# Attention stage: gathered sums copied by ScalarE in two parts, reciprocals on VectorE, multiply on GpSimd

## What is computed

```python
    x = x + _L1_attn_ref(_layernorm(x, axis=-1), L1_attn_w_qkv, L1_attn_w_out, L1_attn_b_out)

    def _L1_attn_ref(x, w_qkv, w_out, b_out):
        ...
        q = q * cos + rotate_half(q) * sin
        k = k * cos + rotate_half(k) * sin
        scale = hd ** (-0.5)
        dots = jnp.einsum('bhid,bhjd->bhij', q, k) * scale
        attn = jax.nn.softmax(dots, axis=-1)
        out = jnp.einsum('bhij,bhjd->bhid', attn, v)
        out = out.transpose(0, 2, 1, 3).reshape(b, n, H * hd)
        return out @ w_out + b_out
```

## Time and profile before

| | |
|---|---|
| median of 3 runs | 2716.94 us |
| lowest and highest | 2711.95 and 2725.21 us |
| profiled execution | 2727.38 us |
| its span | 2725.5 us |
| attention stage, first reduction to last multiply | 979.4 to 1660.0 us |
| busy over the whole span: TensorE, VectorE, ScalarE, GpSimd | 81%, 72%, 52%, 35% |
| largest-value reductions (L2054) | 512, 1.218 us each |
| exponentials (L1918) | 1024, 0.597 us each |

### The profile page before, as it was taken

The page is one execution under the profiler, slowest core; times in us unless marked ns, Lnnn a source line. Parts: engine busy times, 40 slices in busy tenths (PEclk is TensorE's granted clock), DMA queues, the critical chain, the costliest instruction groups (busy, mean ns, idle before and its releaser), DMA issues. The chain is left out here.

```text
span 2725.5 us, 48018 instructions
## 1 busy us (share of the span) xinstructions
PE 2215.1 (81%) x15540; PEld 1397.6 (51%) x15540; DVE 1950.6 (72%) x4482; ACT 1415.7 (52%) x2887; POOL 947.8 (35%) x1183
## 2 busy tenths in 40 slices
PE   3399788876968769999999997959767697698986
PEld 3299577765865312232322323659746686533334
DVE  4466588875656579999999982756567565688893
ACT  2166221214645449989899883336542464533333
POOL 4644335453442321111111100754427444223330
PEclk9999798887989969999999996969978798899998
DMA  5122101001221130000000000112211123100001
GB/s 164 46 58 65 44 18 30 16 22 44 64 82 40 65 128 23 22 20 22 21 21 23 21 3 33 39 51 66 74 44 40 54 63 88 46 0 0 1 0 32
DMA packets 110499, 115.42 MB, mean 42 GB/s; under 512 B 21776, under 2 KB 93552, under 8 KB 109488
## 3 DMA queue, kind: packets, MB, share of 16 engines
q1 hardware_dynamic: 91936, 76.13, 9.8%
q0 software_dynamic: 17280, 35.69, 3.9%
q10 hardware_dynamic: 1040, 0.53, 0.1%
HBM read 67.30 MB, written 44.57 MB: 41 GB/s over the span
## 5 line engine op out<-in xcount | busy, mean ns | idle before, releaser
L2054 DVE TENSOR_REDUCE attn_nm<-bank 128x1 f32<-128x1024 f32 x512 | 592.5, 1218 | 27.2 <-PE bank L1796 24.8
L1918 ACT ACTIVATE attn_pT<-bank 128x512 f32<-128x512 f32 x1024 | 554.3, 597 | 77.3 <-PE bank L1812 70.9
L1831 PE MATMUL bank<-attn_pT,attn_vb 128*32 128x256 f32 x4096 | 334.8, 399 | 10.0 <-issue 10.0
L1796 PE MATMUL bank<-attn_K,attn_Q 48*128 48x512 bf16 x1024 | 317.5, 391 | 23.5 <-PEq L1530 16.7
L1812 PE MATMUL bank<-attn_Q,attn_K 51*128 51x512 bf16 x1024 | 324.5, 390 | 2.0 <-DMA attn_Q<-attn_m_parts 2.0
L1998 POOL CAST attn_m_cols<-attn_nm 128x8 bf16<-128x8 f32 x64 | 12.2, 190 | 483.5 <-DVE attn_nm L2054 455.9
L1831 PEld LDWEIGHTS bank<-attn_pT,attn_vb 128*32 128x32 f32 x4096 | 83.0, 109 | 189.6 <-issue 142.4
L1796 PEld LDWEIGHTS bank<-attn_K,attn_Q 48*128 48x128 bf16 x1024 | 59.4, 94 | 231.1 <-DVE attn_nm L2054 142.8
L2816 POOL TENSOR_TENSOR mix_rS<-mix_rT,mix_S 128x512 f32<-128x512 f32 x64 | 82.7, 1292 | 171.3 <-DVE mix_S L2871 84.4
L1017 PE MATMUL bank<-mix_prod_qk,ident 128*128 128x256 f32 x512 | 124.6, 400 | 0.0
L1017 PEld LDWEIGHTS bank<-mix_prod_qk,ident 128*128 128x128 f32 x512 | 104.4, 204 | 31.8 <-issue 17.7
(11 more groups left out here) (619 smaller groups left out, 5671.2 us busy)
## 6 DMA issues: line engine op xcount, KB each, us to landing
w<-in_L_w SPq DMA_DIRECT2D x4, 2048.0 KB
ffn0a_x_ring<-xs_rows SPq DMA_DIRECT2D x71, 65.0 KB
ffn0b_x_ring<-xs_rows SPq DMA_DIRECT2D x71, 65.0 KB
ffn2a_x_ring<-xs_rows SPq DMA_DIRECT2D x71, 65.0 KB, 1.8
ffn2b_x_ring<-xs_rows SPq DMA_DIRECT2D x71, 65.0 KB, 1.8
mix_in_y_back<-y_rows SPq DMA_DIRECT2D x8, 512.0 KB, 4.0
ffn1a_in_y_back<-y_rows SPq DMA_DIRECT2D x8, 512.0 KB, 4.4
ffn2a_y_back<-y_rows SPq DMA_DIRECT2D x8, 512.0 KB, 3.9
```

Source lines behind the costliest of these rows:

```text
L1796: ins = nc.tensor.matmul(out[:, hf, :], slot(net.Q, h, 0, KROWS)[:, qt * P:(qt + 1) * P], slot(net.K, h, 0, KROWS)[:, hf * CH:(hf + 1) * C ...
L1831: ins = nc.tensor.matmul(pv_bank[at:at + VCOL, cols], vb[:, h, kt, :], q[:, cols], start=(opens(h) and pair == 0 and half == 0), stop=(clo ...
L1918: nc.scalar.activation(pT[:, p_at(b, h, kt), hf * CH:(hf + 1) * CH], s_bank(n), ACT.Exp, scale=HD ** -0.5).then_inc(s_used, 1)
L2054: nc.vector.tensor_reduce(nm[:, v % NMRING, qt:qt + 1], a_bank(n).rearrange("p a t -> p (a t)"), AX.X, ALU.max, negate=True).then_inc(a_us ...
```

## The change

The gather goes in two parts of two tiles each, one at the fifth and one at the sixth tile row, each into a bank of the ring of three (`s_place`) instead of a pair of `big`'s banks. ScalarE copies each part, 128x108, to SBUF (`keep_sums`, into the new tile `gathered`). VectorE takes only the reciprocals, from SBUF, behind the eighth reduction of the head (`invert`, `INVERT_AT` 7). GpSimd multiplies (`over`), behind the split of the maxima and ahead of its other work of that head. `turn_o` waits for GpSimd's multiply. Each step of the sequence's end moves to the next head: 1 and 2, 3 and 4, 4 and 5, 4 and 6, 5 and 7, 6 and 8 where it was 0 and 1, 2 and 3, 3 and 4, 3 and 5, 4 and 6, 5 and 7. The diff, cut to the core; the same shift of heads stands in the programs of TensorE and ScalarE, too:

```diff
--- before.py
+++ after.py
@@ -1646,7 +1646,7 @@
-        TURN_AT, GATHER_AT, END_AT = 4, 4, 6
+        TURN_AT, GATHER_AT, END_AT = 4, (4, 5), 6
@@ -1654,7 +1654,10 @@
-        rd = part.sb("rden", [P, 2, TPB, HEADS_SUMMED])
+        INVERT_AT = GATHER_AT[-1] + 2
+        rd = part.sb("rden", [P, TPB, HEADS_SUMMED])
+        TILES_PART, SUMS_W = TPC // len(GATHER_AT), HPB * SUM_COLS
+        gathered = part.sb("gathered", [P, len(GATHER_AT), TILES_PART * SUMS_W])
@@ -1733,16 +1736,17 @@
-                if kt == GATHER_AT and u > 0 and closes((u - 1) % H):
-                    a_place["sums", *divmod(u - 1, H)] = len(a_place)
+                if kt in GATHER_AT and u > 0 and closes((u - 1) % H):
+                    s_place["sums", *divmod(u - 1, H), GATHER_AT.index(kt)] = len(s_place)
...
-                    if h in (0, 1):
-                        s_place["o", b - 1, h] = len(s_place)
-                    if h in (2, 3):
-                        a_place["y", b - 1, h - 2] = len(a_place)
-                    if h in (5, 7):
-                        s_place["xn", b - 1, h // 7] = len(s_place)
-        a_place["sums", B - 1, H - 1] = len(a_place)
+                    if h in (1, 2):
+                        s_place["o", b - 1, h - 1] = len(s_place)
+                    if h in (3, 4):
+                        a_place["y", b - 1, h - 3] = len(a_place)
+                    if h in (6, 8):
+                        s_place["xn", b - 1, h // 8] = len(s_place)
+        for part_no in range(len(GATHER_AT)):
+            s_place["sums", B - 1, H - 1, part_no] = len(s_place)
@@ -1834,21 +1838,21 @@
-            def gather(b, h):
+            def gather(b, h, part_no):
...
-                if done == 1:
+                if done == 1 and part_no == 0:
...
-                out = take_a(a_place["sums", b, h])
-                W = HPB * SUM_COLS
-                for i in range(TPC):
-                    ins = nc.tensor.matmul(out[:, 0, i * W:(i + 1) * W], sums[:, i * P:(i + 1) * P],
+                out = take_s(s_place["sums", b, h, part_no])
+                for j in range(TILES_PART):
+                    i = part_no * TILES_PART + j
+                    ins = nc.tensor.matmul(out[:, j * SUMS_W:(j + 1) * SUMS_W], sums[:, i * P:(i + 1) * P],
...
-                ins.then_inc(a_ready, 1)
+                ins.then_inc(s_ready, 1)
...
-                pe.wait_ge(a_used, a_place["sums", b, H - 1] + 1)
+                pe.wait_ge(over_step, (b + 1) * len(SPANS))
@@ -1897,14 +1901,15 @@
-                        if kt == GATHER_AT and last and closes(last[1]):
-                            gather(*last)
+                        if kt in GATHER_AT and last and closes(last[1]):
+                            gather(*last, GATHER_AT.index(kt))
...
-            gather(B - 1, H - 1)
+            for part_no in range(len(GATHER_AT)):
+                gather(B - 1, H - 1, part_no)
@@ -1929,8 +1934,15 @@
-                    act.wait_ge(a_ready, a_place["sums", *divmod(u, H)] + 1)
+                    act.wait_ge(s_ready, s_place["sums", *divmod(u, H), len(GATHER_AT) - 1] + 1)
...
+
+            def keep_sums(b, h, part_no):
+                n = s_place["sums", b, h, part_no]
+                need(act, over_step, closed(b * H + h) - 1)
+                act.wait_ge(s_ready, n + 1)
+                nc.scalar.activation(gathered[:, part_no, :], s_bank(n)[:, 0:TILES_PART * SUMS_W],
+                                     ACT.Copy).then_inc(s_used, 1)
@@ -1977,10 +1989,14 @@
+                        if kt in GATHER_AT and last and closes(last[1]):
+                            keep_sums(*last, GATHER_AT.index(kt))
...
+            for part_no in range(len(GATHER_AT)):
+                keep_sums(B - 1, H - 1, part_no)
@@ -2002,16 +2018,27 @@
+            def over(b, h):
+                g, at, size = span(h)
+                pool.wait_ge(inverted, closed(b * H + h))
+                if g == 0 and b > 1:
+                    pool.wait_ge(s_ready, s_place["o", b - 2, HPB - 1] + 1)
+                pv = gathered[:].rearrange("p a (t s e) -> p (a t) s e", s=HEADS_SUMMED, e=V1)[:, :, 0:size]
+                first = first_of[g] * HD
+                nc.gpsimd.tensor_tensor(o[:, b % 2, :, first:first + size * HD].rearrange("p t (s d) -> p t s d", d=HD),
+                                        pv[:, :, :, 0:HD], bcast(rd[:, :, 0:size].rearrange("p t (s a) -> p t s a", a=1),
+                                                                     [P, TPB, size, HD]), ALU.mult).then_inc(over_step, 1)
+
...
-                if h in (2, 3):
-                    add_bias(b, h - 2)
-                if h in (3, 5):
-                    norm.rstd_pow(pool, chunk(b, h // 5))
+                if h in (3, 4):
+                    add_bias(b, h - 3)
+                if h in (4, 6):
+                    norm.rstd_pow(pool, chunk(b, h // 6))
@@ -2054,37 +2084,26 @@
-            def over(b, h):
-                g, at, size = span(h)
-                n = a_place["sums", b, h]
-                chain = Chain(dve, over_step, closed(b * H + h) - 1)
-                dve.wait_ge(a_ready, n + 1)
-                if g == 0 and b > 1:
-                    dve.wait_ge(s_ready, s_place["o", b - 2, HPB - 1] + 1)
-                pv = a_bank(n)[:, 0, 0:TPC * HPB * SUM_COLS].rearrange(
-                    "p (t s e) -> p t s e", s=HEADS_SUMMED, e=V1)[:, :, 0:size]
-                rden = rd[:, g % 2, :, 0:size]
-                chain.then(nc.vector.reciprocal(rden, pv[:, :, :, HD]))
-                chain.wait()
-                first = first_of[g] * HD
-                nc.vector.tensor_tensor(o[:, b % 2, :, first:first + size * HD].rearrange("p t (s d) -> p t s d", d=HD),
-                                        pv[:, :, :, 0:HD],
-                                        bcast(rden.rearrange("p t (s a) -> p t s a", a=1), [P, TPB, size, HD]),
-                                        ALU.mult).then_inc(a_used, 1)
+            def invert(b, h):
+                size, done = span(h)[2], closed(b * H + h)
+                need(dve, over_step, done - 1)
+                dve.wait_ge(s_used, s_place["sums", b, h, len(GATHER_AT) - 1] + 1)
+                pv = gathered[:].rearrange("p a (t s e) -> p (a t) s e", s=HEADS_SUMMED, e=V1)[:, :, 0:size]
+                nc.vector.reciprocal(rd[:, :, 0:size], pv[:, :, :, HD]).then_inc(inverted, 1)
...
-                if qt == END_AT and h in (2, 3):
-                    c, n = chunk(b, h - 2), a_place["y", b, h - 2]
+                if qt == END_AT and h in (3, 4):
+                    c, n = chunk(b, h - 3), a_place["y", b, h - 3]
...
-                if qt == 2 and h in (3, 4):
-                    c = chunk(b, h - 3)
+                if qt == 2 and h in (4, 5):
+                    c = chunk(b, h - 4)
...
-                if qt == 1 and h in (4, 6):
-                    norm.apply(dve, chunk(b, h // 6))
+                if qt == 1 and h in (5, 7):
+                    norm.apply(dve, chunk(b, h // 7))
@@ -2096,12 +2115,12 @@
-                        if qt == GATHER_AT and last and closes(last[1]):
-                            over(*last)
+                        if qt == INVERT_AT and last and closes(last[1]):
+                            invert(*last)
...
-            over(B - 1, H - 1)
+            invert(B - 1, H - 1)
...
```

33 lines of the change are left out of this document (18 added, 15 removed).

## The result

| | before | after |
|---|---|---|
| median of 10 runs each | 2720.77 us | 2734.66 us |
| lowest and highest | 2711.95 and 2727.32 us | 2724.36 and 2737.88 us |
| ratio after to before | | 1.0037, interval 1.0022 to 1.0052 |
| profiled execution, its span | 2727.38, 2725.5 us | 2736.86, 2735.0 us |

The changed kernel is slower by 0.37%, between 0.22% and 0.52%. That is less than the 0.5% within which I had called it the same, but it is not zero: 10 us by this ratio, with 6 to 14 us as its interval. I had worked out 6.7 us.

The account below looks back on a forecast made before the run. The prediction took TensorE's own order as the bound: 24 x (0.14 + 0.05) = 4.6, plus 1.2 and 0.9, is 6.7 us on 2716.94, giving 2724 us. Its 8-in-10 range was 2706 to 2738 us.

Parts of the forecast that it names:

- What bounds the kernel: Attention heads with a gather: TensorE's own order sets the pace, 10.4 of 10.64 us, not waits for VectorE.
- The split: TensorE's gather in two parts: the switch into and out of it is paid twice, +0.14 us per gather.
- ScalarE's ring: Ring of three banks on ScalarE: the two parts as added tenants cost 0, other end 0.29 us per part.
- The reduction after it: Reduction after the gather: fifth tile row's products come earlier, sixth's do not; TensorE's sum unchanged, gain 0.
- The reciprocal: VectorE, behind the eighth reduction: reciprocal from SBUF costs +0.05 us per gather, ends 0 and 0.3.
- GpSimd: GpSimd's multiply of 192 elements takes 0.59 us; work queued behind it keeps nobody waiting, cost 0.
- The sequence end: Statistics moved to the fifth head lose the gather's cover: 0.4 us each for three sequences, 1.2 us.
- The last end: Last sequence's end: copy, handovers and GpSimd's slower multiply stand in the chain uncovered, +0.9 us.
- (a): Rival: VectorE is the bound, each gather gives back 0.76 us, 2699 us in all; chance 0.13.
- (b): Rival: ScalarE's ring becomes the bound at fourth and fifth tile rows, 0.58 us per gather, 2738 us; chance 0.15.
- (c): Rival: copies and waits fall away beside everything, the split pipelines, time stays at 2717 us; chance 0.14.

Follow-up runs that it names:

- e4: Changed kernel without VectorE's reciprocals, GpSimd multiplying numerators by the denominators themselves; ratio to the kernel before 1.0030.
- e6: Kernel before, with VectorE's multiply done a second time into a tile nobody reads; ratio to the kernel before 1.0009.
- e3: Changed kernel with the gather in one part, at the fifth tile row; ratio to the kernel before 1.0028.
- e9: Changed kernel with the gather's two parts one tile row later, at the sixth and seventh; 2716.22 us in one run, kernel before beside it 2699.19 us.
- e5: Kernel before with only the sequence end's six steps moved a head later; ratio to the kernel before 0.9983.
- e8: Kernel before, unedited, profiled a third time; 2719.16 us, timed once.
- e2: Changed kernel, unedited, timed and profiled once more; ratio to the kernel before 1.0036.
- e10: Changed kernel with the whole gather in one part at the sixth tile row; 2714.12 us in one run, kernel before beside it 2699.19 us.

## Why the prediction was right

It said 2724 us, the median came out as 2734.66 us, within its range of 2706 to 2738, and the ratio within the 0.5% called the same. Of those 11 us between forecast and median, 4 are the kernel before, whose median over 10 runs is 2720.77 us and not 2716.94. The change itself costs 13.9 us by the medians and 10 us by the ratio, where 6.7 was foretold; the range had room for that. Term by term the traces show the following.

- **What bounds the kernel: right.** TensorE's own order, not the list of waits. e4 takes everything off VectorE and changes no gather head, and 8.86 + 0.5 + 1.03 us, the prediction's sum for TensorE, is 10.39 of the 10.43 us. What the prediction didn't say is how close the second engine is: e6 puts 0.27 us on VectorE and a gather head pays 0.26, so nothing of it is made good at the stall in the next head, where the prediction had VectorE get 0.2 to 0.3 us back.
- **The split, 0.14 us per gather: right in size.** 0.10 us by the starts of the parts, 0.13 us by e3.
- **ScalarE's ring, 0: mis-sized.** It is 0.08 us by e3, 0.12 us by the pause ahead of the first part. The step that failed: I set the bank's release equal to the end of the exponential ("ends about 1254.6, as the gather is due at 1254.64"), as if the handover took nothing. It takes 0.15 us in the row above. The ring also lent itself to a second error, in the expectations of e9: the 0.28 us of the turn, which the earlier trace rows show for plain heads, had to be somewhere in a gather head, and they were under the gather.
- **The reduction after it: 0, right.** 4.57 us from the fifth tile row's first product to the eighth's (1279.60 to 1284.17), before 4.36 us (1282.55 to 1286.91): 0.21 more, and all of it is in the two terms above.
- **The reciprocal, 0.05 us per gather: right in sum.** It takes 1286.19 - 1285.98 = 0.21 us of VectorE's order, and taking it away gains 1.0 us in heads 1 to 61, 0.05 us for each of 22, though only 0.15 us in the fifth head of each of three sequences, 0.45 us, has a place. In the other gather heads it is covered: VectorE sits idle 1.38 us there after the change. In the kernel before, 0.27 us more on VectorE was not covered (e6).
- **GpSimd, 0: right.** 0.52 us where 0.59 was worked out from its own rows and doubling VectorE's 0.36 us would give 0.72, and nobody waits.
- **The sequence end, 0.4 us each: too much, and for a reason that didn't hold.** The step that failed is "0.76 us of the statistics lay hidden behind TensorE's gather". Beside a second projection in a plain head they hide as well, and 0.09 us was lost. The transposes and the first projection, whose moves I had not priced, gave 0.14 back and took 0.14. In e5 the three sequences together cost 0.2 to 0.5 us in place of 1.2.
- **The last end, +0.9 us: too much.** From the gather to the transposes it is 2.45 us after, and 1.87 us before, by the rows of e8 below: +0.58. The step that failed: I set the multiply of a group of three heads, 0.59 us, against 0.29 us on VectorE, which is the row of a group of two. The last group has two, and its multiply takes 0.41 us on GpSimd: 0.12 us more, and not 0.30.

```profile
1637.69 1.10 PE L1845 MATMUL bank<-attn_pv_sel,attn_sums 128*128 128x54 f32 x8 [0.72 <-ACT attn_sums L1933]
...
1639.56 1.06 PE L1853 MATMUL bank<-ident,attn_o 128*128 128x128 f32 x8 [0.77 <-DVE attn_o L2070]
```

The sum with measured terms is 24 x 0.21 = 5.0 us for the gathers, some 0.45 us for the reciprocal in the fifth heads, 0.2 to 0.5 us for the shift and 0.6 us at the end, 6.3 to 6.6 us. My 6.7 us is close to that by luck: a term too small and two too large nearly cancel. The timed ratio, 6 to 14 us, holds both at its lower edge. What would be above, I can't place. From the last exponential to the next layer it is 21.8 us after and 20.3 in e8, but 21.4 in e5 and 20.5 in e4, so that this varies with the execution.

One thing I had not foreseen makes the ninth head of the third sequence 1.35 and 1.49 us longer in the two profiles of the changed kernel, where e5 and e3 have 0.40 and 0.25 us. All four profiles with the gather in two parts have it (e4 10.73 and e9 10.79 us for that head, e2 10.78), and neither of the two with one part (9.54 us in e3 and e10), so it goes with the split; by what path the split makes the maxima late, no run shows. The next head's first small product waits for the DMA of the maxima (waits between 1400 and 1412 us, total, times, longest):

```profile
PE bank L1816 <- DMA attn_Q<-attn_m_parts: 0.7, 1, 0.7
```

Over the stage such waits of TensorE's loads are 3.4 us in five places after and 3.3 us in four before: they are at other heads, and in sum no more than before. The kernel before has such heads elsewhere: the 11th of the fourth sequence takes 9.75 to 9.87 us in its three profiles and 9.25 us after, the 14th 10.2 to 10.8 us and 9.7 us after.

**The rivals.** (a) falls with e4, though the lack of idle time that spoke for it was real (e6). (b) has the right place and a seventh of the price: one wait of 0.08 us instead of two of 0.29. (c) falls with the interval, which excludes 1.
